# Global attention of an adaLN block on one Trainium2 core: value products in blocks of four steps, with a ring of eight tiles of probabilities

## What is computed

```python
q = _split_heads(x @ Wq + bq, h)
k = _split_heads(x @ Wk + bk, h)
v = _split_heads(x @ Wv + bv, h)
scale = 1.0 / jnp.sqrt(jnp.float32(ATTN_DIM))
pattern = jnp.einsum('bhid,bhjd->bhij', k, q) * scale
prob = jax.nn.softmax(pattern, axis=-2)
out = jnp.einsum('bhis,bhid->bhsd', prob, v)
return concat @ Wo + bo
```

## Time and profile before

| | us |
|---|---|
| median of 3 runs | 5508.29 |
| lowest, highest | 5503.55, 5514.28 |
| the profiled execution's own time | 5510.1 |
| its span | 5508.3 |

### The profile page before, as it was taken

One profiled execution on the slowest core, in us unless ns is written; L12 is line 12 of the kernel. 1 busy time (PEld: TensorE's weight loads), 2 busy tenths in 40 slices (PEclk: granted clock), 3 DMA queues, 4 the chain that ended last, 5 costly groups with the idle time before them and its releaser, 6 DMA issues.

```text
span 5508.3 us, 68426 instructions
## 1 busy us (share of the span) xinstructions
PE 4842.4 (88%) x21552; PEld 2965.5 (54%) x21552; DVE 3788.0 (69%) x4800; ACT 2210.0 (40%) x3328; POOL 2703.6 (49%) x1140
## 2 busy tenths in 40 slices
PE   6899999999997788788859999999999977887878
PEld 3455555555453576676634554554555436665766
DVE  4778778777874664565467777777778756645754
ACT  2334334434333444354323343343344334443543
POOL 0466556555654453355205555556556544533542
PEclk8999999999998899899979999999999988998999
DMA  1000000000001000000010000000000010000000
GB/s 38 5 5 1 5 5 3 3 5 4 2 2 40 16 0 32 16 0 6 26 34 5 5 4 2 5 4 2 5 4 2 2 54 2 0 32 16 0 32 16
DMA packets 78750, 60.28 MB, mean 11 GB/s; under 512 B 41304, under 2 KB 75392, under 8 KB 78208
## 3 DMA queue, kind: packets, MB, share of 16 engines
q1 hardware_dynamic: 78464, 56.50, 3.3%
HBM read 52.02 MB, written 4.19 MB: 10 GB/s over the span
## 4 chain that ended last, share of the span: by engine, by line
POOL 44%; issue 39%; PE 9%; DVE 5%; ACT 1%; POOLq 1%; DMA 1%; DVEq 0%; SPq 0%; ACTq 0%
POOL accp L608 32%; PE psum L1407 4%; POOL lp L630 4%; POOL accp L604 3%; POOL rnorm L620 3%; POOL qk_u L625 2%; DVE lnr L389 1%; PE psum L1420 1%; PE psum L359 1%; PE psum L366 1%; DVE lnc L394 1%; PE psum L1288 1%; POOLq L601 0%; POOL w_low L648 0%; POOLq L606 0%
## 5 line engine op out<-in xcount | busy, mean ns | idle before, releaser
L608 POOL TENSOR_TENSOR accp<-accp,prob 128x1024 f32<-128x1024 f32 x640 | 1596.4, 2494 | 793.5 <-ACT prob L702 759.7
L702 ACT ACTIVATE prob<-psum 128x1024 f32<-128x1024 f32 x1024 | 1041.5, 1025 | 1831.7 <-PE psum L1191 1627.8
L864 DVE TENSOR_REDUCE mx<-psum 128x1 f32<-128x512 f32 x1920 | 1250.3, 686 | 463.9 <-PE psum L1168 427.6
L1202 PE MATMUL psum<-prob,vv 128*64 128x512 f32 x4096 | 994.5, 606 | 0.0
L1190 PE MATMUL psum<-qhh,klh 128*128 128x512 f32 x2048 | 837.8, 409 | 41.2 <-issue 21.4
L1191 PE MATMUL psum<-qlm,kh 65*128 65x512 f32 x2048 | 826.0, 403 | 0.0
L1168 PE MATMUL psum<-klh,qhh 128*128 128x512 f32 x1920 | 720.9, 431 | 73.0 <-DVE mx L864 67.6
L1168 PEld LDWEIGHTS psum<-klh,qhh 128*128 128x128 f32 x1920 | 335.6, 189 | 533.7 <-DVE mx L864 383.0
L1202 PEld LDWEIGHTS psum<-prob,vv 128*64 128x64 f32 x4096 | 249.3, 136 | 513.4 <-issue 391.7
L1190 PEld LDWEIGHTS psum<-qhh,klh 128*128 128x128 f32 x2048 | 396.6, 194 | 209.3 <-issue 99.4
L608 POOL TENSOR_TENSOR accp<-prob 128x1024 f32<-128x1024 f32 x64 | 153.4, 2397 | 701.5 <-ACT prob L702 696.4
(11 more groups left out here) (164 smaller groups left out, 7374.9 us busy)
## 6 DMA issues: line engine op xcount, KB each, us to landing
rot_l<-const_rot SPq DMA_DIRECT2D x6, 2048.0 KB, 8.0
wqkv_l<-L_ffn_wqkv SPq DMA_DIRECT2D x12, 768.0 KB, 9.5
w_l<-L_ffn_w SPq DMA_DIRECT2D x8, 682.0 KB
tok<-L_attn_x SPq DMA_DIRECT2D x32, 128.0 KB, 2.2
out<-tok SPq DMA_DIRECT2D x32, 128.0 KB, 1.7
wo_l<-L_ffn_wo SPq DMA_DIRECT2D x6, 512.0 KB, 10.0
w_l<-L_ffn_w SPq DMA_DIRECT2D x4, 640.0 KB
x<-const_masks SPq DMA_DIRECT2D x2, 1152.0 KB, 5.2
```

Source lines behind the costliest of these rows:

```text
L608: pool.tensor_tensor(acc_p[cp][:], first[:], prob[kt % PRING][:], ALU.add).then_inc(pool_sum, 1)
L702: act.activation(prob[t % PRING][:], psum[:, S_BANK + 2 * (t % 2):S_BANK + 2 * (t % 2) + 2, :].rearrange("p a b -> p (a b)"), ACT.Exp, sca ...
L864: dve.tensor_reduce(mx4[:, j // CHUNKS, j % CHUNKS:j % CHUNKS + 1], ps, AX_X, ALU.max).then_inc(ring_free, 1)
L1202: mm = pe.matmul(psum[j * DH:(j + 1) * DH, O_BANK + cp, :], vv[:, kt, s * DH:(s + 1) * DH], prob[t % PRING][:, j * T:(j + 1) * T], start=( ...
```

## The change

A block has four steps (`VALUES`). In blocks 0 to 6 it is four times scores and a quarter of the block's other pieces, then four value products; the last block has scores 30 and 31, the turn, the projections and four value products. `PRING` is 8, and the four new tiles lie over the buffers of the layer norms, which are not in use in attention. The weights of `max_places` are new: an odd head has 8, 10, 11, 10, 10, 10, 5 and 0 maxima in its blocks, an even one with outputs 9, 8, 9, 11, 11, 11, 5 and 0, and four output items each in blocks 1 and 2.

```diff
--- before.py
+++ after.py
@@ -35,7 +35,8 @@
 KT = N // P
 CP = CHUNKS // 2
 STEPS = CP * KT
-PRING = 4
+PRING = 8
+PLANE = 4
 SUM_DVE = (2, 5, 8, 12)
 SUM_POOL = tuple(k for k in range(KT) if k not in SUM_DVE)
 
@@ -130,6 +131,10 @@
         lns = [sb(f"lns{i}", [P, HALVES, T], at=norms) for i in range(2)]
         norms.close()
 
+        probs_n = ExitStack()
+        prob_n = [sb(f"prob{PLANE + i}", [P, 2 * T], at=probs_n) for i in range(PRING - PLANE)]
+        probs_n.close()
+
         wqkv_h = [sb(f"w{n}_h", [P, HALVES, T], F32R) for n in "qkv"]
         sb("norms_rest", [P, HALVES, T])
         lnr = [sb(f"lnr{i}", [P, T]) for i in range(2)]
@@ -147,7 +152,7 @@
         wv_p = sb("wv_p", [P, HALVES, P], at=att)
         bqk_h = [sb(f"bqk{s}", [P, 1], at=att) for s in range(2)]
         wo_p = sb("wo_p", [P, D], at=att)
-        prob = [sb(f"prob{i}", [P, 2 * T], at=att) for i in range(PRING)]
+        prob = [sb(f"prob{i}", [P, 2 * T], at=att) for i in range(PLANE)] + prob_n
         acc_p = [sb(f"accp{i}", [P, 2 * T], at=att) for i in range(CP)]
         acc_d = [sb(f"accd{i}", [P, 2 * T], at=att) for i in range(CP)]
         rcp = sb("rcp", [P, T], at=att)
@@ -260,22 +265,25 @@
 
 
 
-        GROUPS = STEPS // 2
-        SUM0_GROUP = (KT + 5) // 2
+        VALUES = 4
+        GROUPS = STEPS // VALUES
+        SUM0_GROUP = (KT + 5) // VALUES
+        OUT_GROUPS = 2
+        OUT_EACH = WO_ITEMS // OUT_GROUPS
 
         def max_places(outs):
 
 
-            weight = [4] * (GROUPS - 1) + [0]
-            weight[0] = 1
-            weight[SUM0_GROUP + 1:SUM0_GROUP + 3] = [0, 2]
+            weight = [8] * (GROUPS - 1) + [0]
+            weight[0] = 6
+            weight[SUM0_GROUP + 1] = 4
             for g in outs:
-                weight[g] = 3
+                weight[g] = 6
             return [-(-RING_MAX * sum(weight[:g + 1]) // sum(weight)) for g in range(GROUPS)]
 
         def head_order(first, last, hh):
             maxima, projects = not (last and hh), not last
-            outs = () if first or hh else range(1, 1 + WO_ITEMS // 2)
+            outs = () if first or hh else range(1, 1 + OUT_GROUPS)
             placed = max_places(outs)
             order = [("scores", 0), ("scores", 1)]
             for g in range(GROUPS):
@@ -283,19 +291,19 @@
                 done = (placed[g - 1] if g else 0) if maxima else 0
                 tiles = [("max", j) for j in range(done, upto)]
                 if g in outs:
-                    tiles += [("out", 2 * (g - 1)), ("out", 2 * (g - 1) + 1)]
-
-                n = len(tiles)
-                cut0 = (n + 1) // 3
-                cut1 = cut0 + n // 3
+                    tiles += [("out", OUT_EACH * (g - 1) + j) for j in range(OUT_EACH)]
+
                 if g + 1 < GROUPS:
-                    order += tiles[:cut0] + [("scores", 2 * g + 2)] + tiles[cut0:cut1] + [("scores", 2 * g + 3)] + tiles[cut1:]
+                    for j in range(VALUES):
+                        order.append(("scores", VALUES * (g + 1) - 2 + j))
+                        order += tiles[len(tiles) * j // VALUES:len(tiles) * (j + 1) // VALUES]
                 else:
+                    order += [("scores", STEPS - 2), ("scores", STEPS - 1)]
                     if maxima:
                         order.append(("turn", 0))
                     if projects:
                         order += [("proj_qk", i) for i in range(QK_ITEMS)]
-                order += [("values", 2 * g), ("values", 2 * g + 1)]
+                order += [("values", VALUES * g + j) for j in range(VALUES)]
                 if g == SUM0_GROUP:
                     order.append(("sum", 0))
             if projects and hh == 1:
```

## The result

| | before | after |
|---|---|---|
| median, us | 5505.92 (4 runs, 5501.0 to 5514.28) | **5886.78** (4 runs, 5880.86 to 5887.01) |
| ratio | | 1.0687, interval 1.0669 to 1.0706 |
| profiled execution: time, span, us | 5510.1, 5508.3 | 5886.6, 5884.8 |

The change costs 381 us. The forecast was 5903, 16 us too high. The program's lines moved: maxima are L1176 now (L1168), scores L1198 and L1199, value products L1210, sums L1219, projections L1156 and L1168; on DVE L872 reduces, L889 adds, L895 divides.

What follows compares the result with a forecast made beforehand. PE's own sequence was taken to bound attention, with DVE next. Terms 210 + 2 + 112 + 7 + 28 + 36 = 395 us on the profiled 5510.1, which stands 2 above the median, gave 5903 us; range 5740 to 5990.

Steps and rivals of the forecast that it cites:

- Drains, -90: PE entering and leaving half-width value products: 0.35 us a block, 8 fewer blocks in each of 32 heads, 90 us less.
- Blocks 1 to 5: Odd heads' middle blocks, runs of three maxima held by two PSUM tiles: 11.45 us with 10 maxima, 12.49 with 11.
- Rival 3: Runs of three maxima in blocks 1 to 5 cost nothing, only the second sum waits: 5636 us, 13%.
- The second sum, +112 and +7: Head's end: PE waits for DVE's late step 28 addition, 8.0 us in 14 even heads (+112), 0.5 in odd (+7).
- Rival 2: The second sum's wait is hidden, for instance by DVE done sooner; only ring and block 6 remain: 5756 us, 12%.
- Clock after that pause, +28: Half clock on second sum and next scores after the even head's wait: 2 us in 14 heads, ends 0 and 56.
- Block 6 and the odd head: PE pauses 2.5 us while DVE divides, block 6 ends 12.45 us behind the first sum; odd head +7.0 us altogether.
- The clock drop of +36: Lower clock after block 6's pause: 1.2 us in each of thirty heads, +36 us, ends 0 and 60.
- rival 4: As forecast but without a clock drop in block 6: 5867 us, 25%.
- Even heads: Even head from start to the end of its values: 107.2 us against 100.2, +7.0 us.
- The ring at nothing: Eight tiles of probabilities add no work and no exponential needs more than six: no cost.
- Last heads, +1 each: A batch's two last heads, without maxima: exponentials hold four scores in a row about 0.5 us, +1 us each.

Runs made afterwards that it cites:

- experiment 8: Kernel of experiment 6 with maxima dealt singly between the sixteen score matmuls of a block (last eight in blocks 0 and 6): 5441.89 us, ratio 0.9885.
- experiment 9: Kernel before the change, blocks of two steps, with maxima spread singly among eight score matmuls: 5461.1 us, ratio 0.9917.
- experiment 2: Changed kernel with a block's maxima cut in five parts, the first ahead of the first score, so no run of three: 5787.96 us, ratio 1.0517.
- experiment 1: Changed kernel with DVE's addition for step 28 moved ahead of the turn, not behind the four projection items: 5810.89 us, ratio 1.0559.
- experiment 4: Kernel before the change with only the ring of probabilities raised from four to eight tiles: 5506.85 us, ratio 1.0003.
- experiment 6: Kernel of experiment 5 with the maxima of blocks 0 and 6 moved to the last three fifths of the block: 5558.05 us, ratio 1.0094.
- experiment 3: Changed kernel with the edits of experiment 1 and experiment 2 together: 5713.72 us, ratio 1.0385.
- experiment 5: Kernel of experiment 3 with a head's first sum put ahead of block 5's values, not behind them: 5589.76 us, ratio 1.0151.

## Why the prediction was right, and where it was not

**Drains, -90: right in size, though never to be had alone.** Values of a block of four take 3.59 us with the way out (700.83 to 704.42), and 3.70 with the 0.11 before the next matmul is at pace; 3.67 was forecast. With 0.10 on the way in it is 3.80, where two old blocks took twice 0.10 + 1.86 + 0.11, that is 4.14: 0.34 for each block saved. The Trainium skill, TensorEngine Tiling (Array Packing), Key Properties, says that a change of tiling mode drains the engine. The trace agrees with it by these 0.34 us. Best against best, experiments 8 and 9, blocks of four are 19 us faster than blocks of two, not 90. Where the other 71 went I have not separated; block 0, block 6 and the heads' ends are the places left.

**Blocks 1 to 5: right.** 11.46 and 12.58 against 11.45 and 12.49. Three constants of one block of the trace before were enough. Rival 3 (threes cost nothing) falls; experiment 2 gets 1.1 us a block back by the cuts alone, as the constants say. The Trainium skill, TensorEngine Tiling (Array Packing), PSUM Bottleneck, says that tiling speeds up TensorE but not the emptying of PSUM. The traces agree: a reduction on DVE took 686 ns before and 687 after, on the mean of the two pages (L864, L872). But its load was not the limit, since DVE had 63 us of every 200 to spare. It was not too slow, it was asked in bunches, with two banks to hold them. Whether ScalarE could take some of the reductions was not tried.

**The second sum, +112 and +7: mechanism right, size a little over.** 7.1 us of wait, not 8.0, since the sum followed the start of an addition that took 1.23 us, not the 1.79 of the earlier trace rows, by 6.19 us and not 6.77, and since block 7 itself took 13.20 us, not 12.84. (Its term 0.70 + 0.59 + 1.03 is 2.32, not the 2.4 written; the trace has 2.55.) In odd heads nothing was visible in place of 0.5. Before the last pair's odd head the wait was 5.07, where 4.13 stood before. That the lateness came from DVE's queue is shown by experiment 1. Rival 2 (hidden) falls.

**Clock after that pause, +28: right.** The sum took 0.95 us more, and its next four matmuls 1.85 us where 1.04 is the pace: 1.8 of the 2 us. The reason given, that DVE's division covers the rest, was not needed in this head, since the half clock ended by itself after 3.8 us. In five of the 14 heads it lasted 5.6 to 6.6 us behind the sum's start, and the next values came only 0 to 0.5 us later, so there it held.

**Block 6 and the odd head: the size right, the shape wrong.** Values of block 6 started 8.57 behind the sum (8.8 forecast), the block ended 12.16 behind it (12.45). Block 0 of the odd head took 13.4 us (13.6). I counted only that DVE was busy. The bank of the sum is itself one of the two, which splits the pause into 1.15 and 0.80. The clock drop of +36 is the term that was over-sized: it came in 12 of 30 heads, 1.5 us each, 18 us together. So the forecast, which has it in all, and rival 4, which has it in none, are both half right, and their totals lie on either side, 16 us too high and 20 too low.

**Even heads: +9.8, not +7.0.** This is the term that made up for the clock drops that did not come. Timeline and window of PE at the start of one:

```profile
607.61 0.47 PE L1198 MATMUL psum<-qhh,klh 128*128 128x512 f32 x1 [3.13 <-issue]
...
623.12 0.50 PE L1198 MATMUL psum<-qhh,klh 128*128 128x512 f32 x1
```

```profile
609.00:616.00 7.00, 7.00 (x18) 5.09 (x17) 2.53 (x5) 4.07 (x4) 2.39 (x2) 0.51 0.09 18
```

Block 0 took 15.5 us (13.9 forecast): the half clock lasted 7 us, where the earlier trace rows had shown 3, and I had carried the 3 over. Blocks 1 and 2 took 15.8 each (15.2, 15.5), since the first output item waits for DVE as a maximum does. From there on the head is as forecast up to the end of block 6, which comes 49.7 us later, and 49.7 was written.

**The ring at nothing: right** in the old order, by experiment 4; in the new one nothing separates it. **Last heads, +1 each: right.** A block took 8.14 us in place of 7.88 for two old ones, but the whole head, second sum to second sum, grew by 1.5 and 0.6 us only.

**Additions at about 1 us: read too widely.** That hold stands only in the 14 heads with output items, where the addition took 3.15 us; in the other 16 the blocks behind an addition took about 5.65 us, 0.55 over the rest. The forecast put it at nothing in the new order, so its total did not hang on it.

So the total was hit within 16 us partly because errors cancel. In the pair shown, even heads took 2.8 us more than written; the clock in block 6 (2.4), the wait (0.9) and the odd head (0.9) took 4.2 less. The balance of one pair can't be taken 16 times: only 14 even heads have output items, and 12 heads have the clock drop. But the signs stay: even heads cost more than written, the clock in block 6 cost 18 us less, and the two profiled sums differ by 395 - 376 = 19.

## What to carry to other kernels

Blocks of one kind of matmul may be merged only as far as the items between them stay evenly spread: a drain of 0.35 us is lost again by one third item in a row before a ring of two. Before moving a block's border, follow each engine's queue past it, since an addition that slips behind a series of projections was a fifth to a third of this loss (76 of 381 us came back in experiment 1, some 8.9 us in each of 14 heads are spent in the trace), and a wait that is taken away can come back at the next place where the same engine is late. Where a list of pieces is dealt out by hand, deal them singly: in blocks of four that alone gave 116 us (experiment 6 to 8). In blocks of two it gave 45, but nearly all of that through an addition that met another engine's at a better moment, so look for what became shorter before giving the new order the credit.

## What was not expected of the hardware

The granted clock does not follow from one pause alone. In the change, block 6 of nearly all of the 30 heads has the same two pauses, 1.15 to 1.17 and 0.79 to 0.81 us, and 12 of them went on at half clock, 18 did not. (The last pairs' even heads have a second pause of 1.15; one fell, one did not.) In experiment 1 it is 12 and 18 again, for the most part other heads. With first pauses of 2.1 us there (experiments 2 and 3) the clock fell in all 30 heads; with one pause of 1.0 (experiment 5) in none. After 7.1 us at the sum PE went at the half clock for 3.8 us behind it in the head shown, and after 3.13 us at the start of a loop for 7. A forecast should carry such a term with both ends, as a part of its range, and one head shown can't tell which end it is.

An addition on DVE and one on POOL that overlap did not share the cost evenly. Where DVE's started 0.3 us behind POOL's it took 3.15 us and POOL's 2.37; where it started 0.07 ahead it took 1.22 and POOL's 3.38 (experiment 9). A shift of POOL's start by 0.4 us took 1.9 us off DVE's addition and put 1.0 on POOL's.
